# Attention scores computed twice, the second time with keys on partitions, in place of transposed probabilities

## What is computed

```python
x = x + tanh(g_xattn[0]) * attention0(layernorm(x), ctx, ctx)     # 16 heads of 8 dims, softmax over 64 keys
x = x + tanh(g_ffn[0])   * experts0(layernorm(x))                 # 8 experts, best 2 of each token
x = x + tanh(g_xattn[1]) * attention1(ctx, ctx, layernorm(x), mask)
x = x + tanh(g_ffn[1])   * experts1(layernorm(x))                 # 4 dense experts, gated

scores = einsum('bhqd,bhkd->bhqk', q, k) * scale                  # d = 8
probs  = softmax(scores, axis=-1)
out    = einsum('bhqk,bhkd->bhqd', probs, v)
```

## Time and profile before

| | |
|---|---|
| runs | 1438.8, 1426.07, 1433.82 us; median 1433.82 |
| profiled execution, first to last instruction (span) | 1173.7 us |
| median less that span | 260.1 us |
| PE matmul busy | 1095.9 us, 93% |
| PE weight loads busy | 930.7 us |
| VectorE / ScalarE / GpSimd busy | 902.1 / 715.9 / 543.8 us |

### The profile page before, as it was taken

One profiled execution on the slowest core, in us unless ns is written; L12 is line 12 of the kernel. 1 busy time (PEld: TensorE's weight loads), 2 busy tenths in 40 slices (PEclk: granted clock), 3 DMA queues, 4 the chain that ended last, 5 costly groups with the idle time before them and its releaser, 6 DMA issues.

```text
span 1173.7 us, 39887 instructions
## 1 busy us (share of the span) xinstructions
PE 1095.9 (93%) x13589; PEld 930.7 (79%) x13589; DVE 902.1 (77%) x3189; ACT 715.9 (61%) x1565; POOL 543.8 (46%) x699
## 2 busy tenths in 40 slices
PE   6899999999984899999999799999999979999998
PEld 4777777777762899999999577777777768999997
DVE  4778878889887454554543699999999979988886
ACT  4777778777760555555555577777777744444443
POOL 2112565556757334344443866666666421222230
PEclk7999999999996899999999899999999999999999
DMA  7223311111202333333333222222222100000000
GB/s 199 71 79 92 92 56 54 54 55 55 68 29 83 90 94 95 93 96 96 94 95 84 56 50 52 49 48 48 51 50 50 24 2 10 27 18 26 18 18 28
DMA packets 116781, 71.88 MB, mean 61 GB/s; under 512 B 51737, under 2 KB 105241, under 8 KB 116633
## 3 DMA queue, kind: packets, MB, share of 16 engines
q1 hardware_dynamic: 108440, 53.13, 16.8%
q0 software_dynamic: 8192, 16.79, 4.8%
HBM read 45.88 MB, written 22.94 MB: 59 GB/s over the span
## 4 chain that ended last, share of the span: by engine, by line
PE 69%; DVE 8%; ACT 7%; issue 7%; POOL 4%; SPq 2%; DMA 2%; DVEq 0%; ACTq 0%; POOLq 0%
PE ps_m L1741 11%; PE ps_m L1518 8%; PE ps_p L1506 7%; PE ps_s L1468 5%; PE ps_p L1622 5%; PE ps_m L1622 4%; PE ps_s L1478 4%; PE ps_s L1727 3%; PE ps_s L1728 3%; PE ps_s L1729 3%; ACT Kbd L749 3%; PE ps_m L1494 2%; ACT Pr L739 2%; PE ps_s L1610 2%; PE ps_s L1611 2%
## 5 line engine op out<-in xcount | busy, mean ns | idle before, releaser
L970 DVE TENSOR_REDUCE mx<-ps_s 128x8 f32<-128x512 f32 x256 | 168.7, 680 | 36.7 <-PE ps_s L1468 36.3
L1518 PEld LDWEIGHTS ps_m<-Vbd,PT 128*64 128x64 f32 x4096 | 137.8, 138 | 48.4 <-issue 42.8
L709 ACT ACTIVATE PT<-ps_p 128x512 f32<-128x512 f32 x256 | 152.7, 597 | 27.0 <-PE ps_p L1506 24.8
L1518 PE MATMUL ps_m<-Vbd,PT 128*64 128x18 f32 x4096 | 158.2, 213 | 0.2 <-ACT PT L709 0.2
L786 ACT ACTIVATE Kbd<-ps_s,c 128x512 f32<-128x512 f32 x128 | 87.3, 688 | 114.5 <-PE ps_s L1612 114.5
L1506 PE MATMUL ps_p<-cst,Pr 128*128 128x128 f32 x1024 | 155.2, 280 | 0.4 <-DVE orow L1246 0.4
L572 POOL TENSOR_TENSOR spare<-spare 1x1 f32<-1x1 f32 x99 | 21.1, 213 | 285.4 <-DVE b1s L1329 146.0
L648 POOL DMA_INDIRECT w1a<-louts,gi x128 | 125.5, 980 | 38.6 <-issue 29.5
L1741 PE MATMUL ps_m<-xn3T 128*128 128x128 f32 x1136 | 138.0, 275 | 0.2 <-ACT xn3T L851 0.2
L1741 PEld LDWEIGHTS ps_m<-xn3T 128*128 128x128 f32 x1136 | 132.7, 192 | 0.4 <-issue 0.4
L851 ACT ACTIVATE xn3T<-ps_s,b1s 128x256 f32<-128x256 f32 x284 | 111.2, 474 | 26.1 <-PE ps_s L1729 26.0
(11 more groups left out here) (219 smaller groups left out, 2695.8 us busy)
## 6 DMA issues: line engine op xcount, KB each, us to landing
xn3T<-lists SPq DMA_DIRECT2D x71, 128.0 KB, 2.1
louts<-xn3T SPq DMA_DIRECT2D x71, 128.0 KB, 1.9
ctxg<-in_ctxT SPq DMA_DIRECT2D x32, 256.0 KB
Kbd<-in_ctxT SPq DMA_DIRECT2D x512, 8.0 KB
out<-x SPq DMA_DIRECT2D x16, 256.0 KB, 2.3
w1a<-in_L_ffn_W SPq DMA_DIRECT2D x8, 256.0 KB, 3.3
w2a<-in_L_ffn_W SPq DMA_DIRECT2D x8, 256.0 KB, 4.0
Pr<-in_ctxT SPq DMA_DIRECT2D x16, 128.0 KB, 2.4
```

The costliest lines, as they stand in the source:

```text
L709: return nc.scalar.activation(dst, src, ACT.Copy)
L970: V.tensor_reduce(mx[g.par][:, q, :], per_key(ps_s[:, q, :]), AX, ALU.max).then_inc(max_done, 1)
L1518: ins = mm((bank7, bank6)[pr][S * b:S * b + S, VW * j:VW * (j + 1)], PT[c][:, P * i + S * b:P * i + S * b + S], Vbd[g.par][:, 2 * pr + b, ...
```

## The change

Scores are made twice per group. Both passes use matmuls of 8 contraction rows (one head) instead of 32 rows of a block-diagonal tile:

- **Queries and keys in rows of eight dims.** The projection weights are permuted so that each 32-partition quarter of the result holds dim by head; ScalarE copies it to `stage`, and SyncE's DMAs put it into `qk`: partition 32q + d, then head of the quarter, then side (query, key), then 256 tokens. Layer 0 issues four such DMAs a group; layer 1 eight, since its keys come from a DRAM copy of the context, `keys`, which layer 0 writes (one DMA a group).
- **First scores**, queries on partitions, 64 matmuls of 64 x 64 a group in two halves, into banks 0 and 1 of `ps_s`. VectorE takes only their negated maxima, two reductions of 128x1024. TensorE turns them (one 128x128), ScalarE copies 32 rows out, and two DMAs of SyncE put them into `qk` as one more contraction row, against a row of ones beside the keys. In layer 1 the mask is one more row too (one DMA).
- **Second scores**, keys on partitions: again 64 matmuls of 64 x 64, with 9 rows (10 in layer 1), into banks 2 and 3, with minus the maximum already in. ScalarE exponentiates 128x1024 twice, straight from PSUM.
- **Values**: no transposes and no copies of probabilities. `probs_by_values` becomes 128 matmuls: 64 rows, 32 queries as weights, 9 moving columns (8 dims and a one for the denominator), in two row halves and four column quarters.
- Gone: `Kbd`, `Vbd`, `PT`, `subtract`, `less_maximum`, high and low maxima, the mask matmuls, 16 transposes and four copies a group. Reciprocals and products become one instruction each. In layer 1 the four normalising instructions move from VectorE to ScalarE, with `nb` (minus mean times inverse deviation) made on VectorE. The logits and values become two full matmuls in place of eight halves.
- The pipeline is one stage deeper at each end: s = -5 to 36. Banks are shared anew: outputs, heads, maxima, logits and ranks use `ps_p`, the rest `ps_m`.

The core of the diff:

```diff
-            for s in range(-4, GROUPS + 4):
+            for s in range(-5, GROUPS + 5):
...
+            def queries_in(g, half):
+                i = g.k % QK
+                sp.wait_ge(q_staged, g.count(1, 1))
+                wait(sp, st_done, g.count(2, 1 - 2 * QK + half))
+                for q in (2 * half, 2 * half + 1):
+                    part, rows = slice(32 * q, 32 * q + 32), slice(32 * q, 32 * q + ROWS)
+                    if g.layer == 0:
+                        sp.dma_start(qk[i][rows, :, :, :], stage[g.par][part, :, :]).then_inc(q_in[half][i], 16)
...
+            def maxima_in(g):
+                r = MAXROW[g.layer]
+                sp.wait_ge(mt_ready, g.count(1, 1))
+                for u in range(2):
+                    sp.dma_start(qk[g.k % QK][r:r + 97:32, :, 0, P * u:P * u + P],
+                                 mxT[g.par][u:31 + u:2, :]).then_inc(mx_in[g.par], 16)
...
+            def exps(g, half):
+                act.wait_ge(st_done, g.count(2, half + 1))
+
+                wait(act, pv_done, g.count(1, -1))
+                nc.scalar.activation(Pr[g.par][:, 2 * half:2 * half + 2, :], ps_s[:, 2:4, :], ACT.Exp,
+                                     scale=SCALES[g.layer]).then_inc(exp_done, 1)
...
+            def maximum(g, half):
+                dve.wait_ge(s_done, g.count(2, half + 1))
+
+                wait(dve, mt_done, g.count(1, -1))
+                V.tensor_reduce(mx[g.par][:, 16 * half:16 * half + 16],
+                                ps_s[:, 0:2, :].rearrange("p a (n k) -> p (a n) k", k=S), AX, ALU.max,
+                                negate=True).then_inc(max_done, 1)
...
+            def scores(g, half):
+
+
+                own, turned = g, g.plus((-2, -1)[half])
+                other = 1 - half
...
+                for u in range(2):
+                    for h in range(HB):
+                        for i in range(2):
+                            token = slice(P * u + S * i, P * u + S * i + S)
+                            side = slice(S * i, S * i + S)
+                            col = slice(S * (2 * h + u), S * (2 * h + u) + S)
+                            end = (u, h, i) == (1, HB - 1, 1)
+                            if own.real():
+                                src = qk[own.k % QK]
+                                for r in range(2):
+                                    q = 2 * half + r
+                                    rows = slice(32 * q, 32 * q + ROWS + own.layer)
+                                    ins = mm(ps_s[side, r, col], src[rows, h, 0, token], src[rows, h, 1, token],
+                                             start=True, stop=True, skip_group_check=True)
+                                if end:
+                                    ins.then_inc(s_done, 1)
+                            if turned.real():
+                                src = qk[turned.k % QK]
+                                for r in range(2):
+                                    q = 2 * other + r
+                                    rows = slice(32 * q, 32 * q + ROWS + 1 + turned.layer)
+                                    ins = mm(ps_s[side, 2 + r, col], src[rows, h, 1, token], src[rows, h, 0, token],
+                                             start=True, stop=True, skip_group_check=True)
+                                if end:
+                                    ins.then_inc(st_done, 1)
...
+                for h in range(HB):
+                    for q in range(4):
+                        head = HB * q + h
+                        for u in range(2):
+                            for r in range(2):
+                                for i in range(2):
+                                    side = slice(S * i, S * i + S)
+                                    col = S * (2 * h + u) + 32 * r
+                                    ins = mm(ps_p[64 * u + 32 * r:64 * u + 32 * r + 32, i, VW * head:VW * head + VW],
+                                             Pr[g.par][side, q, col:col + 32], Vo[g.par][side, u, head, :],
+                                             start=True, stop=True, skip_group_check=True)
                 ins.then_inc(pv_done, 1)
...
                 if g.layer == 0:
-                    now(probs_turned, -1, 0)
+                    scores(g, 0)
+                    if g.k == -2:
+                        pe.wait_ge(consts_done, 1)
+                    now(logits, -4)
+                    now(project_out, -3)
+                    if g.k == 0:
+                        pe.wait_ge(setup_in, SETUP)
+                    now(values, -1)
+                    now(keys_queries, 2)
+                    now(probs_by_values, -2)
+                    scores(g, 1)
+                    now(tokens2_turned, -3)
                     now(heads_turned, -2)
...
+                    now(tokens_turned, 3)
+                    block = router_due(g, -5, 0)
+                    if block:
+                        ranks(block, g)
+                    now(maxima_turned, 0)
```

More of the change, by code:

```diff
@@ L1187, in step @@
[L1187 to L1188 removed]
+                    now(maximum, 0, 0)
+                    now(router_logits, -4)
+                    now(residual, -3)
+                    if g.k > LATE_SUMS:
+                        now(late_sum, -2)
+                    now(statistics_mid, -3)
+                    now(moments, -3, 0, lnf_st, lnf_mv, xn2_ready)
+                    if g.k - 4 in AT_ONCE:
+                        first_choice(g.plus(-4))
+                        second_choice(g.plus(-4))
+                        both_choices(g.plus(-4))
@@ new lines, in step @@
+                else:
+                    now(statistics_in, 3)
+                    now(moments, 3, 2, lnq_st, lnq_mv, xn_ready)
+                    now(combine, 4)
+                    now(gate_logits, -4)
+                    now(residual, -3)
+                    now(statistics_mid, -3)
+                    now(moments, -3, 0, lnf_st, lnf_mv, xn2_ready)
+                    now(maximum, 0, 0)
+                    now(gate_hidden, -4)
+                    if have(-3) or have(3):
+                        means_scaled(g)
+                    now(denominators, -2)
+                    now(heads, -2)
+                    now(gate_depth, -4)
+                    now(maximum, 0, 1)
+                    if g.k == GROUPS + 2:
+                        dve.wait_ge(pv_done, LAST.count(1, 1))
@@ L1483, in tokens_turned, with maxima_turned @@
+            def maxima_turned(g):
+                pe.wait_ge(max_done, g.count(2, 2))
+                if g.plus(-2).real():
+                    pe.wait_ge(on_ready, g.plus(-2).count(1, 1))
+                else:
+                    wait(pe, mt_ready, g.count(1, 0))
+                turn(mt_bank, mx[g.par][:, :], ident).then_inc(mt_done, 1)
             def tokens_turned(g):
-                bank_free(pe, 7, g.plus(-1), "XT")
+                if g.layer == 0 and g.plus(-4).real():
+                    pe.wait_ge(v_ready, g.plus(-4).count(1, 1))
+                else:
+                    wait(pe, xnT_ready, g.count(1, 0))
@@ L1685, in step @@
+                else:
+                    scores(g, 0)
+                    now(logits, -4)
+                    now(project_out, -3)
+                    now(keys_queries, 2)
+                    now(probs_by_values, -2)
+                    scores(g, 1)
+                    now(tokens2_turned, -3)
+                    now(heads_turned, -2)
+                    now(tokens_turned, 3)
+                    now(maxima_turned, 0)
                     experts_first(g)
             def experts_first(g):
-                if g.k == GROUPS:
+                if g.k == GROUPS + 1:
```

796 lines of the change are left out of this document (339 added, 457 removed).

## The result

| | median us | beside before | ratio, 95% interval |
|---|---|---|---|
| changed kernel | 1878.68 | 1436.31 | 1.3112, 1.3057 to 1.3167 |
| the same on another chip (after_b) | 1753.76 | 1178.48 | 1.488 (one run) |

The forecast was 1390 us. The kernel is 442 us slower instead of 44 faster.

A forecast was written before the change was run, and what follows sets the result against it. PE, busy 93% of 1173.7 us, bounds layer 1, a ring through all engines layer 0. Savings of 22 and 40 us less 18 for the ends leave about 1130; 260 us outside the span makes 1390, range 1345 to 1490.

The forecast's parts named there:

- the four small-matmul parts: Two halves each of first and second scores, and probs_by_values, on PE: 512 matmul records and 512 loads, 4.4 us a step.
- Small matmuls at 4.3 ns an instruction: PE's scores and probs_by_values: 1024 instructions at 4.3 ns over runs of 256 and 512, 4.4 us a step.
- The first rival's second form: PE's instruction queue: each 16 KB block waits 2.4 us to land, 10.1 us a step, 1478 us; chance 0.27 for both forms.
- Lower clock in emptier steps: PE's clock in both layers: one of three hand-over losses, together 0.7 us a step more, 1433 us; chance 0.12.
- the third rival: Hand-overs between engines eat the gain: late query DMA, ScalarE's longer exponentials or lower clock, 0.7 us a step, 1433; chance 0.12.
- Second scores and turns lie beside VectorE's 2.45 and are hidden: Layer 0: PE's second scores and three pairs of transposes (1.05 + 0.9 us) add nothing; up to 0.5 without that cover.
- The 260 us outside the span are left as they are: Whole kernel: the median of 1433.82 us is 260 above the profiled span; that part was kept unchanged and unexplained.
- GpSimd's floor of 7.4 us in layer 1: Layer 1: GpSimd's gathers and powers need about 7.4 us a step, the next bound just under PE's 7.85.
- The second rival: PE's small matmuls do not run eight abreast: 512 cost 18.6 us, 14.2 more a step, 2270 us; chance 0.08.
- the fourth rival: Column quarters work too in probs_by_values on PE: 1.2 us instead of 2.3, 1345 us in all; chance 0.08.

The follow-up runs named there:

- Micro: Four stretches of 1024 small matmuls each, values and scores, looped and written out, added to the kernel before ahead of the experts; 1630.71 us.
- micro_b: The same added looped and written-out stretches of small matmuls in the kernel before, run once more on a faster chip; 1363.88 us.

## Why the prediction was wrong, point by point

The step that failed is the price of the four small-matmul parts: 1024 instructions at 4.3 ns, 4.4 us a step, with everything else beside them at the full clock. The runs show at least 3.45 us per 256 written-out instructions and 1.2 GHz for such matmuls. In after_b, the first half of scores, `probs_by_values` and the second half of scores alone take 2.1 + 4.8 + 4.5 = 11.4 us.

- **"Small matmuls at 4.3 ns an instruction"**: right at the full clock and from a full buffer (4.2 ns, 479 in 2.00 us), at half clock 4.6 for the values (256 in 1.2 us) and 7.6 for the scores (256 in 1.95 us). Wrong in the length of run it was taken over: the burst of the earlier trace rows was 18 instructions, and a step has 1024.
- **The first rival's second form is what happened, mis-sized.** It had the mechanism, blocks of 16 KB each waiting for a landing of 2.4 us, and priced it at 2.4 us a block, 10.1 us a step. Measured: 2.3 to 2.9 us from the packet to the first instruction, but the packet itself comes 1.1 us or more behind the start of the block before, so 3.45 at least and 4.26 in the mean in layer 1 of after_b. 4.2 x 4.26 = 17.9 us a step; 4.2 x 3.45 = 14.5 would already have made it slower than before. The missing term is that in these rows the next block's packet never comes before the present block has begun. The earlier trace rows had only 10 packets in 80.8 us, too sparse to show it.
- **"Lower clock in emptier steps"** was one of three items in a bracket of the third rival, at 0.12, with 1433 us. It is the second large term, and it isn't emptiness: PE without a gap in small matmuls is at 0.50. Logits to queries cost 4.6 us instead of the forecast's 2.9 (0.5 + 0.61 + 0.5 + 1.26), the first half of scores 2.1 instead of 1.05.
- **"Second scores and turns lie beside VectorE's 2.45 and are hidden"**: they took 4.5 and 1.3 us, with a hole of 2.2 us without an instruction. VectorE was through with its other work at 269.5 us and idle for 2.84 us, until these scores let its second maximum begin:

```profile
272.36 1.23 DVE L1012 TENSOR_REDUCE mx<-ps_s 128x16 f32<-128x1024 f32 x1 [2.84 <-PE ps_s L1469]
```

- **"The 260 us outside the span are left as they are"**: nothing lies outside. Spans and times agree within 2 us in every run that has both (1876.7 and 1878.4). The 260 us are longer steps of the kernel before on a slower chip. Micro's part of the unchanged kernel shows it: 10.1 us a step early in layer 0, 15.3 later, 11 to 19 in layer 1, the clock at 0.76 here:

```profile
1000.00:1100.00 100.00, 94.82 (x973) 67.72 (x973) 62.30 (x227) 48.57 (x105) 42.75 (x56) 0.76 0.13 32
```

  How much of it is the lower clock and how much the delay beside the gathers (the `scores` of 2.8 us above, at the full clock) isn't separated.

- **GpSimd's floor of 7.4 us in layer 1** was occupation, and what binds is the ring through its gathers, 11.2 to 11.8, with nothing of PE in it. The changed kernel hides it under 18 us. The second rival (tiles not abreast) and the fourth (eight tiles abreast, 1345) are settled for their rates: at 4.2 ns the values' 512 instructions would take 2.15 us at the full clock, against the forecast's 2.3 and the fourth rival's 1.2.

In sum, on a chip like that of the profile: forecast 1130 us, measured 1752.0; 62 steps x (18.0 - 8.7) = 577 of the 622 us.

## What to carry to other kernels

Count the instructions that PE has to be given in a pipeline step and multiply by the block interval: written-out code brought 256 instructions in 3.45 us at best here, and splitting the matmuls four- to eightfold moved the bound from the array to that queue. Before costing a stage at the full clock, find a stretch with the same size of matmul and read its granted clock, since a full row of busy tenths didn't mean the full clock here. And when a median and a span differ by a fifth, settle why before building on either.

## What was unexpected of the hardware

- Blocks of 256 of PE's written-out instructions (`probs_by_values` alone) began 3.46 to 4.01 us apart in the rows of micro_b, and alike in micro on a slower chip, at half clock in both, with PE idle for 2.0 to 2.6 of them.
- 34 us of gapless matmuls of 8 rows and 64 columns were granted 0.50, and in that test the clock was 1.00 only behind full matmuls.
- The same kernel took 1177 us on some chips and 1436 on others, and only on the latter did PE's instructions trickle, about 10 per 0.75 us, beside GpSimd's indirect DMAs; removing the gathers removed the trickle (some 20 times in layer 1, to none). On the slower chips the kernel before's own `scores` took 2.8 us instead of 1.1 beside the gathers, at the full clock.
